# Four items by batch at the end of the first layer, and the first projection rows in that layer's block

## What is computed

```python
x = x + 0.5 * _L0_ffn_ref(_layernorm(x, axis=-1), ...)
x = x + _L0_attn_ref(_layernorm(x, axis=-1), ...)
x = x + 0.5 * _L0_ffn_ref(_layernorm(x, axis=-1), ...)

# in the ffn: each expert takes its 256 best tokens of each batch
topk_w, topk_idx = jax.lax.top_k(scores, cap)
x_tok = jnp.take_along_axis(hidden_states[:, None, :, :], topk_idx[..., None], axis=2)
g = jnp.einsum('becd,efd->becf', x_tok, Wg)
u = jnp.einsum('becd,efd->becf', x_tok, Wu)
h = jax.nn.gelu(g, approximate=False) * u
eo = jnp.einsum('becf,edf->becd', h, Wd) * topk_w[..., None]
flat = flat.at[flat_idx].add(eo.reshape(-1, d))
# in the attention
q = x @ Wq.T + bq
k = x @ Wk.T + bk
v = x @ Wv.T + bv
q = apply_rope(q)
k = apply_rope(k)
```

## Time and profile before

| | us |
|---|---|
| median of 3 runs | 1497.94 (1497.44 to 1500.55) |
| the profiled execution | 1495.94 |
| its span | 1494.2 |
| TensorE busy | 1460.3 (98%) |
| ScalarE busy | 1085.6 (73%) |
| VectorE busy | 894.1 (60%) |
| GpSimd busy | 565.2 (38%) |
| the 40 matmuls on ones, start and length | 457.55, 2.41 |
| first matmul behind the boundary | 460.26 |
| last matmul of the projections, start | 545.25 |

### The profile page before, as it was taken

The page is one execution under the profiler, slowest core; times in us unless marked ns, Lnnn a source line. Parts: engine busy times, 40 slices in busy tenths (PEclk is TensorE's granted clock), DMA queues, the critical chain, the costliest instruction groups (busy, mean ns, idle before and its releaser), DMA issues. The chain is left out here.

```text
span 1494.2 us, 26723 instructions
## 1 busy us (share of the span) xinstructions
PE 1460.3 (98%) x9935; PEld 1022.7 (68%) x9939; DVE 894.1 (60%) x1984; ACT 1085.6 (73%) x1391; POOL 565.2 (38%) x485
## 2 busy tenths in 40 slices
PE   5999999999999999999999999999999999999998
PEld 4788888888897773334343343333788888888887
DVE  7888777677667971222145052126788867776774
ACT  7322277777746889999999999999622247777772
POOL 5000357766646961202111121111300045666645
PEclk9999999999999999999999999999999999999999
DMA  8212388898846799505336062221511158878873
GB/s 306 78 57 71 88 221 182 190 193 201 194 73 183 253 281 182 88 1 87 57 86 131 30 130 52 37 68 61 162 53 63 57 166 184 205 178 195 193 164 43
DMA packets 180403, 195.74 MB, mean 131 GB/s; under 512 B 77297, under 2 KB 142321, under 8 KB 177521
## 3 DMA queue, kind: packets, MB, share of 16 engines
q1 hardware_dynamic: 152096, 146.30, 39.5%
q0 software_dynamic: 28176, 47.73, 14.9%
HBM read 123.73 MB, written 55.57 MB: 120 GB/s over the span
## 5 line engine op out<-in xcount | busy, mean ns | idle before, releaser
L2513 ACT ACTIVATE 6375_pr<-6375_pS 128x1024 f32<-128x1024 f32 x448 | 420.5, 1192 | 2.0 <-PE 6375_pS L2408 2.0
L2439 PE MATMUL 6375_pO<-6375_pr,6360_vres 128*32 128x512 f32 x1792 | 237.3, 603 | 0.0
L2408 PEld LDWEIGHTS 6375_pS<-sq_rows,sk_rows 50*128 50x128 f32 x896 | 77.3, 183 | 177.5 <-ACT 6375_pr L2513 133.5
L2408 PE MATMUL 6375_pS<-sq_rows,sk_rows 50*128 50x512 f32 x896 | 183.3, 467 | 1.1 <-ACT 6375_prs L2513 0.8
L351 PE MATMUL 6386_pGU<-columns_ahead,weights_wts 128*128 128x512 f32 (+1 forms) x400 | 155.5, 389 | 0.3 <-DVE 6386_hf L1297 0.2
L2537 POOL TENSOR_SCALAR_AFFINE_SELECT 6375_pr<-6375_pr 128x512 f32<-128x512 f32 x32 | 20.3, 636 | 356.4 <-ACT 6375_pr L2513 356.4
L352 PE MATMUL 6386_pGU<-columns_ahead,weights_wts 128*128 128x512 f32 (+1 forms) x400 | 152.6, 381 | 0.0
L353 PE MATMUL 6386_pGU<-columns_ahead,weights_wts 128*128 128x512 f32 (+1 forms) x400 | 152.4, 381 | 0.0
L351 PE MATMUL 93_pGU<-columns_ahead,weights_wts 128*128 128x512 f32 (+1 forms) x368 | 143.1, 389 | 1.6 <-issue 1.3
L1106 ACT ACTIVATE hidden_hT<-93_hf 128x512 fp32r<-128x512 f32 x96 | 60.7, 632 | 112.7 <-DVE 93_hf L1297 112.7
L352 PE MATMUL 93_pGU<-columns_ahead,weights_wts 128*128 128x512 f32 (+1 forms) x368 | 140.1, 381 | 0.0
(11 more groups left out here) (441 smaller groups left out, 3588.0 us busy)
## 6 DMA issues: line engine op xcount, KB each, us to landing
93_raw_g<-WgT SPq DMA_DIRECT2D x16, 512.0 KB, 4.0
93_raw_u<-WuT SPq DMA_DIRECT2D x16, 512.0 KB, 4.2
93_raw_d<-WdT SPq DMA_DIRECT2D x16, 512.0 KB, 5.3
q_rows<-rows_halves SPq DMA_DIRECT2D x8, 1024.0 KB, 5.0
k_rows<-rows_halves SPq DMA_DIRECT2D x8, 1024.0 KB, 5.1
6386_raw_g<-WgT SPq DMA_DIRECT2D x16, 512.0 KB, 3.6
6386_raw_u<-WuT SPq DMA_DIRECT2D x16, 512.0 KB, 3.7
6386_raw_d<-WdT SPq DMA_DIRECT2D x16, 512.0 KB, 4.8
```

Of the source, the lines that this page charges most:

```text
L2408: m = t_.matmul(to[:, e, :], key, query, start=True, stop=True)
L2439: m = t_.matmul(pO[e * 32:(e + 1) * 32, j % 2, off:off + wd], vres[:, (g // GB) * TPB + kt, at:at + 32], from_(e), start=n == first[j], st ...
L2513: s_exp.done(a.activation(to, pS[:, u % RING, :, :], ACT.Exp, scale=HD ** -0.5))
```

## The change

Four items (20 to 23) are mixed instead of three: experts 12 and 13, then 14 and 15, each pair first for batch 0 and then for batch 1. All items from 8 on use four places for weights, and a new table `splits` spreads the conversions: three a step, and a fourth in steps 12, 14, 16, 18 and 20; three in step 21 and one in 22. The steps up to 23 all take the general order, in which the evacuation of a down projection's first half comes ahead of the lowering of the next columns.

The first quad is loaded once item 21's scatters have landed, the second behind it. Both are normalised in the first block, with their statistics in step 24 between VectorE's other work. The first quad is turned and the first two blocks of its rows are made in that block, in banks that both blocks now share; the matmuls on ones are gone. ScalarE loads the table for the square root between the last gelu and the last high half. The bias is loaded ahead too. In the projections TensorE, ScalarE and VectorE leave out what is made; GpSimd's queue is as it was but for what its clear of `sk` waits for.

```diff
-WARM = 40
+        PLACES = 4
+        FOURTH = range(J + 4, J + 14, 2)
             def slot(s):
-                if lead and s >= NI - 2:
-                    return s - NI + 4
+                if lead and s >= J:
+                    return (s - J) % PLACES
                 return 1 if s < J else s % 2
             def parts(item):
-                if lead and e >= E - 3:
-                    return (((E - 3, 0), (E - 2, 0)), ((E - 1, 0), (E - 3, 1)), ((E - 2, 1), (E - 1, 1)))[e - E + 3]
+                if lead and e >= E - PLACES:
+                    one, b = E - PLACES + 2 * (e % 2), (e - E + PLACES) // 2
+                    return (one, b), (one + 1, b)
+            def splits(s, at):
+                ahead = 3 * (s - J) + sum(x < s for x in FOURTH)
+                return [(J + n // 3, n % 3) for n in range(ahead, min(3 * E, ahead + 3 + (s in FOURTH)))][at:at + 1]
@@ on_sync
                 if lead:
                     self.load_projection_weights(sp)
+                    self.counter("proj_const", 16).done(sp.dma_start(self.row_bias[:, :], self.ins["b_rows"]))
                     s_wl.wait(sp, 3 * E)
-                    for k in range(2):
-                        s_so[k].wait(sp, J // 2 + 1)
+                    s_sc[(NI - 3) % 2].wait(sp, (E - 3) // 2 + 1)
                     for q in range(2):
+                        if q == 1:
+                            s_U.wait(sp, 4 * (NI - 1))
@@ on_tensor
+                def turn_lead():
+                    t_.wait_ge(*s_xn.at(J + 1))
+                    t_.wait_ge(*s_rowed.at(2))
+                    for c in range(DC):
+                        for j in range(4):
+                            m = t_.transpose(pGU[:, c, j * P:(j + 1) * P], self.lead_x[0][:, j, c * P:(c + 1) * P], self.ident[:, :])
+                def rows_lead():
+                    t_.wait_ge(*s_xl.at(DC * (NI + 1)))
+                    for n in range(2):
+                        for c in range(DC):
+                            m = self.product3(t_, pGU[:, 2 + n, :], self.lead_w[0][:, c, cols], self.lead_w[1][:, c, cols], ...)
                 def last_down(d):
+                        if q == 2:
+                            turn_lead()
-                    for _ in range(WARM):
-                        t_.matmul(pG(0)[:, 0:P], self.ones[:, :], self.ones[:, :], start=True, stop=True)
+                    rows_lead()
@@ on_scalar
+                    gelu(s, 3)
+                    if lead and s == NI:
+                        a.activation(warm[:, :], self.eps[0:1, :], ACT.Sqrt)
+                    high(s, 3)
+                    s_std.done(a.activation(std[:, :, :], mv[:, :, :, 1], ACT.Sqrt, bias=self.eps[:, :]))
+                    s_xn.done(lead_rows(0, (2, 3)))
+                    lead_rows(1, (0,))
+                    for c in range(DC):
+                        s_xh.done(a.activation(self.turned_x[0][:, 0, c, :], pGU[:, c, :], ACT.Copy))
+                    s_xn.done(lead_rows(1, (1, 2, 3)))
@@ on_vector
                 def last_steps(s):
                     if s == NI + 1:
-                        lead_statistics()
-                        evacuate_last(NI - 1)
+                        lead_scale()
+                        evacuate_last(NI - 1, range(3))
+                        lead_low_columns()
+                        evacuate_last(NI - 1, (3,))
                         return
                     mul(s, 0)
+                    low(s, 0)
+                    evacuate(s, 0)
+                    lead_statistics(0)
+                    evacuate(s, 1)
+                    s_wl.done(v.tensor_tensor(self.lead_w[1][:, :, :], self.qkv_raw[:, :, :], ...))
+                    for f in range(1, FC):
+                        mul(s, f)
+                        if f == 1:
+                            lead_statistics(1)
+                        low(s, f)
@@ projections
+                s_T.bump(t_, DC)
+                s_Q.bump(t_, 2)
                 for q in range(J):
-                    if q == 0:
-                        first_rows()
-                    else:
+                    if q >= 1:
                         rows(4 * q)
-                    rows(4 * q + 1)
+                        rows(4 * q + 1)
@@ on_gpsimd
-                        if lead and item == NI - 3 and q == 2:
+                        if mixed(item) and q == 2:
                             s_sc[k].wait(g, e // 2 + 0.5)
                     if n == 0:
-                        g.wait_ge(*s_xn.at(2))
+                        g.wait_ge(*s_T.at(2 * DC))
```

More of the change, by code:

```diff
@@ L389, in load_constants @@
                        for q in range(2)]
+        self.turned_x = [nc.alloc_sbuf_tensor_at(f"turned_x{h}", [P, 2, DC, 4 * P], self.f32r, offset=self.stage_at + (48 + 8 * h) * 1024)
+                         for h in range(2)]
         self.eo = nc.alloc_sbuf_tensor_at("eo", [P, 2, 4, D], self.f32, offset=self.stage_at + EO_AT)
@@ L541, in parts @@
                 e = item - J
-                if lead and e >= E - 3:
-                    return (((E - 3, 0), (E - 2, 0)), ((E - 1, 0), (E - 3, 1)), ((E - 2, 1), (E - 1, 1)))[e - E + 3]
+                if lead and e >= E - PLACES:
+                    one, b = E - PLACES + 2 * (e % 2), (e - E + PLACES) // 2
+                    return (one, b), (one + 1, b)
                 return (e, 0), (e, 1)
-            mixed = lambda item: lead and item >= NI - 3
+            mixed = lambda item: lead and item >= NI - PLACES
+            def splits(s, at):
+                if not lead:
+                    return [(s, w) for w in range(3)][at:at + 1]
+                ahead = 3 * (s - J) + sum(x < s for x in FOURTH)
+                return [(J + n // 3, n % 3) for n in range(ahead, min(3 * E, ahead + 3 + (s in FOURTH)))][at:at + 1]
             number = lambda s, f, h: 4 * (s - 1) + f + (4 * h if h else 0)
@@ L930, in last_down @@
                     s_ev.wait(t_, 2 * d)
-                    for q in range(2):
+                    for q in range(3):
                         for c in range(FC - 1):
@@ L935, in last_down @@
                     for q in range(4):
-                        for c in range(FC - 1 if q < 2 else 0, FC):
+                        for c in range(FC - 1 if q < 3 else 0, FC):
                             m = rows_down(d, q, c, own_bank(q))
                         s_Dq.done(m)
+                        if q == 2:
+                            turn_lead()
                 def last_row(d, q, chunks):
@@ L1113, in split, with split_at @@
                             s_stored[k].wait(a, kept[k])
-                    elif slot(item) >= 2:
+                    elif lead and J + 2 <= item < J + PLACES:
                         s_U.wait(a, 4 * J)
                     elif w < 2:
-                        s_U.wait(a, 4 * (item - 1))
+                        s_U.wait(a, 4 * (item - (PLACES - 1 if lead and item >= J + PLACES else 1)))
                     else:
-                        s_D.wait(a, 2 * (item - 1))
+                        s_D.wait(a, 2 * (item - (PLACES - 1 if lead and item >= J + PLACES else 1)))
                     split_hi(a, slot(item), w)
+                def split_at(s, at):
+                    for item, w in splits(s, at):
+                        split(item, w)
                 if ready:
@@ L1572, in scatter @@
                                                     None, compute_op=ALU.add)
-                        if item == NI - 2 and q < 2:
+                        if not lead and item == NI - 2 and q < 2:
                             s_so[q].done(sent)
@@ L1751, in rows @@
                     s_Q.done(m)
-                def first_rows():
-                    cols = slice(0, P)
-                    for c in range(DC):
-                        t_.wait_ge(*s_xh.at(c + 1))
-                        for h in range(2):
-                            t_.matmul(pQ[:, 0, :], w[h][:, c, cols], xT[0][:, 0, c, :], start=(c, h) == (0, 0), stop=False)
-                    for c in range(DC):
-                        t_.wait_ge(*s_xl.at(c + 1))
-                        m = t_.matmul(pQ[:, 0, :], w[0][:, c, cols], xT[1][:, 0, c, :], start=False, stop=c == DC - 1)
-                    s_Q.done(m)
                 def values(q, halves=range(2)):
@@ L2687, in attn @@
             self.s_ld = [[sig(f"loaded{k}{pair}", 16 * 10) for pair in range(2)] for k in range(2)]
-            project, shift, attend = self.projections(st, x), self.exact_shift(), self.attention(x, out)
+            project = self.projections(st, x)
+            self.kept.close()
+            shift, attend = self.exact_shift(), self.attention(x, out)
             return [project, shift, attend]
```

246 lines of the change are left out of this document (108 added, 138 removed).

## The result

| | before | after |
|---|---|---|
| median of 20 runs | 1497.95 (1497.40 to 1500.55) | 1500.34 (1499.36 to 1506.19) |
| profiled execution, span | 1495.94, 1494.2 | 1500.02, 1498.3 |
| mean granted TensorE clock in it | 0.999 | 0.997 |

The ratio of the runs is 1.0021, 95% interval 1.0014 to 1.0027: slower by 2.4 us where 1.9 was forecast, a small difference that lies clear of its interval. The two profiled executions differ by 4.1 us, more than the medians; where the rest comes from is part of what follows.

A forecast was written before the change was run, and what follows sets the result against it. TensorE's own matmuls were taken to set the first layer's pace, GpSimd's queue the work behind the boundary. +1.8 at the boundary plus 0 behind it gave 1497.7 profiled, plus 2.0 to the median 1499.8 us; range 1495.8 to 1503.2.

The forecast's parts named there:

- Parts 1 and 2: Four mixed items remove waits in steps 21 and 22, starting step 24 2.0 us earlier; first quad there at 442.2.
- Part 3: Step 24: VectorE stops for the quad; TensorE stands 2.4 us before the last down projection, losing the 2.0 and 0.4 more.
- Part 4: Last down projection to the boundary between the blocks: boundary moves from 460.26 to 462.05, +1.8 us.
- The table load: ScalarE behind the last gelu: 1.28 us plus 0.20 activation; with the skill page's drain, boundary at some +2.9.
- Part 5: Behind the boundary: 3.7 us leave TensorE, but GpSimd's queue holds the projections; gain 0, upper bound 3.7.
- The 2.0 us between profile and median: Whole kernel: median of runs lies 2.0 above the profiled execution, so 1497.7 becomes 1499.8.
- Rival C: TensorE idle about 4.4 us before its first norms, clock falls to 1.2 GHz: 0 to 6 us, put at 2; chance 0.12.
- the forecast's likeliest case: Whole kernel as summed, +1.8 us at the boundary and 0 behind it, 1499.8 us; chance 0.43.
- A: Step 24: quad or TensorE in time, boundary -0.6, 1497.3; chance 0.22 for A or B in part, 0.09 both whole.
- B: Behind the boundary GpSimd does not hold projections; half of 3.7 kept, 1497.9; A or B in part 0.22, both whole 0.09.
- E: Steps 21 and 22: the waits stay though the conversions are moved, +2.6 us, 1502.4; chance 0.04.
- D: Later chain in step 24: 6.8 us flight, +2.0; or fourth conversions stall, +7.5 at most; chance 0.10.

The follow-up runs named there:

- after: The changed kernel as first measured and profiled, against the kernel before: median 1500.34 us, ratio 1.0021.
- items_only: Kernel before with only the items part (four mixed items, places, conversions, first quad's load); normalising, turning, rows and 40 filling matmuls as before: 1493.57 us, 0.9979.
- pool_first: Changed kernel with GpSimd's first sum of turned rows ahead of its wait for the first late scatters and the second pair: 1497.18 us, 1.0007 of before.
- filled kernel: Changed kernel with matmuls on ones where TensorE stands, 36 ahead of the last down projection, 52 ahead of the first norms: 1497.73 us, 1.0010 of before.
- trig_late: Changed kernel with the trigonometric table's four transfers (2 MB) held back until the last down projection's second row block is done: 1501.38 us, 1.0019 of before.
- after_again: The changed kernel measured and profiled a second time, nothing edited: 1499.38 us, 1.0022 of the kernel before on the same chip.
- stats_later: Changed kernel with the first quad's statistics behind the second evacuation and the projection weights' low half on VectorE: 1497.95 us.
- items_no_fill: Kernel before with the items part alone, and also without its 40 filling matmuls (`WARM = 0`): 1494.41 us, 0.9985 of before.

## Why the prediction was right, and where only its total was

The total was +1.8; between the two profiles without the late releases the attention begins 1.7 later, the span is 1.9 longer (ScalarE's first exponential, before, then after's second profile):

```profile
549.02 1.94 ACT L2513 ACTIVATE 6375_pr<-6375_pS 128x1024 f32<-128x1024 f32 x2 [1.23 <-PE 6375_pS L2408]
```
```profile
550.75 1.94 ACT L2528 ACTIVATE 6441_pr<-6441_pS 128x1024 f32<-128x1024 f32 x2 [1.27 <-PE 6441_pS L2423]
```

But the +1.8 is made up otherwise than I had it, and that it came out is luck: the boundary came 1.25 us later than I had it, and GpSimd's first sum 1.3 us closer behind it.

**Parts 1 and 2 held.** From the gelu at 376.44 to the one at 435.82 the kernel before takes 59.4 us, the changed kernel in its first profile 57.35 (377.51 to 434.86): 2.0 shorter, as forecast. (The 1.7 and 1.1 of part 1 are spacings with the regular 0.23 and 0.12 in them; without those 2.5 are left, near the 2.6 that I took.) And the five steps with a fourth conversion take 16.66 us as before, so it costs nothing. In the second profile item 21's first scatter goes at 425.77 (424.6), the quad's load at 437.97 (437.4), its statistics start at 442.93 (442.2). The flight was 5.0, in the first profile 5.75: within the bounds named.

**Part 3 held**: the last down projection begins at 452.34 (451.9) behind 2.43 us of idle time (2.4).

**Part 4 was too low by 1.25**: 463.31, that is +3.05, where I had 462.05, +1.8. TensorE's timeline of after's second profile, the start of the last down projection, of the rows, and the first matmul behind the boundary:

```profile
452.34 0.38 PE L350 MATMUL 95_banks<-columns_wts,hidden_hT 128*128 128x256 f32 x1 [2.43 <-DVE hidden_hT L1346]
...
459.46 0.47 PE L350 MATMUL 95_banks<-turned_x,lead_w 128*128 128x512 f32 x1 [0.24 <-DVE turned_x L1450]
...
463.31 0.47 PE L350 MATMUL 95_banks<-turned_x,lead_w 128*128 128x512 f32 x1 [0.89 <-DVEq L69]
```

0.4 was there already, 0.1 came in the 36 matmuls; the term that failed is the crossing, "the last matmul's end and 0.3 for the boundary as before". It took 0.89, that is 0.6 more, and the wait for the low columns 0.1 more than I had. My reading is that before, filling matmuls for which nobody waited stood last and hid part of the meeting of the engines, and now products stand last. No run tests that by itself: the kernel with the items alone has the filling and still waits 0.6. The table load took 1.28 and the small activation 0.20, with no drain of 1380 ns between them (after: 453.53, 454.82), as the row and not the page of the Trainium skill (ScalarE: Activation LUTs, What ACT_TABLE_LOAD costs) had it.

**Part 5 was right in its mechanism and too high by 1.3 in its size.** GpSimd does hold the projections: it works without a pause from its first sum for ten instructions, and VectorE's ninth block waits 1.27 us for it:

```profile
473.50 2.93 POOL L2024 TENSOR_TENSOR 6435_turn_pair<-6435_turn_pair 128x1024 f32<-128x1024 f32 x1
...
499.07 2.40 POOL L2024 TENSOR_TENSOR 6435_turns<-6435_turns 128x1024 f32<-128x1024 f32 x1 [0.40 <-DVE 6435_turns L1947]
...
489.41 0.75 DVE L1941 SCALAR_TENSOR_TENSOR 6435_turn_pair<-95_banks,49_row_bias,trig 128x512 f32<-128x512 f32 x1 [1.27 <-POOL rows_halves L2028]
```

(GpSimd, then VectorE, in after's second profile; the fellows of the earlier trace rows.) But "it reaches its first sum 11.5 us behind the boundary" took the landing for a fixed length. It is 10.2: GpSimd starts 0.3 sooner behind TensorE's first matmul, and the landing is 5.0 instead of 6.1. The quads' and the table's 3 MB, issued from 449.6 on in the kernel before, are through by then, which is the likely cause (T4). The sum as measured: 3.05 - 0.3 - 1.05 = +1.7.

**The 2.0 us between profile and median** were a term as well, added to get 1499.8. They have the size of the late releases: the first profile of before is free of them and lies 2.0 us under its median, the first of after has them and lies 0.3 under its own. That they are the reason is my reading; the runs without a profile don't show it.

**Rival C came true**, which the forecast's likeliest case left out: the granted clock falls, in both traces of the changed kernel under GpSimd's work, as I reckoned for part of it, and in a variant (`pool_first`) at a place where it costs 1.5 us. By the medians of the filled kernel it is worth some 1.5 us (I had put it at 2 if it came). The chance of 0.12 was too low: the idle piece it hangs on, which I counted as 4.4 us, was 3.4, and was certain by my own part 5. Also unforeseen are the 0.3 us of the third layer. Against the median of before on the same chip the changed kernel stands at +2.9 in one measurement and +2.4 in the other: 1.7 + 0.3 are traced, the rest I put down to the clock.

Rivals A, B and E did not come; of D only the flight, in part.

## What to carry to other kernels

Ask of an edit with two parts what each does alone: here one gave 2.9 us, and the other took more than 5 away by the medians. In the traces the changed kernel's boundary is 4.7 us later than with the items alone: 2.4 in which TensorE waits for VectorE, which stood for the quad, and most of the rest for turning and rows, put ahead of a point behind which GpSimd's queue let nothing start sooner. A statement "the queue starts x behind the boundary" needs its transfers taken apart: a landing was 5.0 to 7.2 us here, and loads moved back to it lengthened it by 2.1. Idle time of TensorE cost little by itself here and, by the medians, more through its clock; filling it cost nothing that the trace shows.

## What the runs showed of the hardware

- TensorE's clock fell to half for 3.4 us (6.8 in `trig_late`) around the end of waits of 1.9 us (`pool_first`) and 3.4 to 3.6 us (`after`, `after_again`, `stats_later`, `trig_late`), starting between 1.2 us before that end and 0.7 behind it, and not at waits of 2.8 (`items_no_fill`), 2.7 and 2.4 us. It cost 1.5 us in `pool_first`, where matmuls were on the path, and nothing visible in the other traces. Its place moved between variants that differ little.
- Two scatters of late rows landed in 5.0 us on DMA engines that were idle just before (`after_again`: 0.00 from 458 to 464), and in 7.2 with 2 MB of loads issued from 9 us before the second one (`trig_late`). Without such loads they still took 5.3 in one variant and 6.5 in another (`items_only`, `items_no_fill`).
- In five of fourteen profiles VectorE was released 2.8 us behind the end of the matmuls that it waited for, at the same place in the program, in both kernels, at some 1 us a time: in all four from two of the chips, in none of the eight from a third. The profile names no cause.
